# Macaron block on one Trainium2 core: a prologue put in another order, with two width tests

## The reference

```python
x = x + 0.5 * ffn(layernorm(x), ...)
x = x + mixer(layernorm(x), ...)
x = x + 0.5 * ffn(layernorm(x), ...)      # the same weights

def ffn(x):
    h = (x - mean(x)) * rsqrt(var(x) + 1e-5) * gamma + beta
    y = silu(h @ w1 + b1)                  # 256 -> 1024
    return x + 0.5 * (y @ w2 + b2)         # 1024 -> 256
# w1 and w2: (q - 128) * scales, q int32, one scale per 128 rows and column

def mixer(x):
    a = sigmoid(x @ Wa + ba); b = x @ Wb + bb; c = tanh(x @ Wc + bc)
    s[t] = a[t] * s[t-1] + (1 - a[t]) * b[t]
    return (c * s) @ Wy + by + (x @ Wd + bd)
```

## Time and profile before

| what | value |
|---|---|
| median of 3 runs | 690.57 us (689.08 to 690.64) |
| profiled execution, its own time | 690.4 us |
| its span in the profile | 687.6 us |
| granted TensorE clock over the span | 0.999 |
| TensorE, ScalarE, VectorE, GpSimd busy | 97%, 95%, 92%, 88% of the span |
| first product of fc1 on TensorE | 16.94 us |
| first scaling on ScalarE | 18.74 us |
| first product of fc2 | 25.78 us |

### The profile page before, as it was taken

The page is one execution under the profiler, slowest core; times in us unless marked ns, Lnnn a source line. Parts: engine busy times, 40 slices in busy tenths (PEclk is TensorE's granted clock), DMA queues, the critical chain, the costliest instruction groups (busy, mean ns, idle before and its releaser), DMA issues.

```text
span 687.6 us, 13669 instructions
## 1 busy us (share of the span) xinstructions
PE 668.0 (97%) x3224; PEld 539.2 (78%) x3224; DVE 634.8 (92%) x1329; ACT 653.4 (95%) x1095; POOL 604.8 (88%) x673
## 2 busy tenths in 40 slices
PE   3999999999999999999999999999999999999997
PEld 3678888888888878778877887788888888888885
DVE  5789999999999999889999998899999999999987
ACT  4899999999999999889999999999999999999994
POOL 4899999999999999857766789999999999999973
PEclk9999999999999999999999999999999999999999
DMA  8670000000000000000000000000000000000001
GB/s 254 172 236 4 1 0 0 0 0 0 0 0 0 1 0 2 1 1 1 0 0 0 0 1 1 30 33 32 31 31 31 31 31 31 31 31 32 32 32 63
DMA packets 19962, 20.22 MB, mean 29 GB/s; under 512 B 1564, under 2 KB 19666, under 8 KB 19922
## 3 DMA queue, kind: packets, MB, share of 16 engines
q1 hardware_dynamic: 19824, 19.74, 9.3%
q10 hardware_dynamic: 98, 0.02, 0.0%
HBM read 11.37 MB, written 8.39 MB: 29 GB/s over the span
## 4 chain that ended last, share of the span: by engine, by line
PE 90%; ACT 3%; DVE 3%; issue 2%; DMA 1%; ACTq 0%; POOL 0%; DVEq 0%; POOLq 0%
PE ps_z L1009 38%; PE ps_fc L1009 33%; PE ps_fc L1142 8%; PE ps_tr L1002 5%; PE ps_tr L1070 4%; PE ps_fc L1150 2%; PE ps_z L1002 1%; DMA rows<-in_L_attn_bc 1%; DVE z_acc L762 1%; ACT ps_fc L576 1%; ACT g_hi L593 1%; DVE stats L699 1%; ACT g_full L591 0%; DVE resid L887 0%; ACTq L530 0%
## 5 line engine op out<-in xcount | busy, mean ns | idle before, releaser
L410 POOL TENSOR_TENSOR g_lo<-g_full,g_hi 128x512 fp32r<-128x512 f32 x256 | 332.9, 1300 | 24.7 <-ACT g_hi L593 21.8
L762 DVE SCALAR_TENSOR_TENSOR z_acc<-ps_z,cols,z_acc 128x512 f32<-128x512 f32 (+1 forms) x449 | 322.2, 742 | 24.2 <-PE ps_z L1009 16.4
L1009 PE MATMUL ps_fc<-h_hi,q_sb 128*128 128x512 f32 x512 | 213.4, 417 | 1.4 <-ACT ps_fc L576 1.4
L1009 PE MATMUL ps_z<-g_hi,q_sb 128*128 128x512 f32 x512 | 202.4, 395 | 0.1
L1009 PE MATMUL ps_fc<-h_lo,q_sb 128*128 128x512 f32 x512 | 202.3, 395 | 0.0
L1009 PE MATMUL ps_z<-g_lo,q_sb 128*128 128x512 f32 x512 | 200.6, 392 | 0.0
L591 ACT ACTIVATE g_full<-ps_fc,safe_scale 128x512 f32<-128x512 f32 x256 | 194.8, 761 | 3.9 <-PE ps_fc L1009 2.2
L593 ACT ACTIVATE g_hi<-ps_fc,safe_scale 128x512 fp32r<-128x512 f32 x256 | 196.2, 766 | 0.0
L576 ACT ACTIVATE ps_fc<-ps_fc,bias,ratio 128x512 f32<-128x512 f32 x193 | 157.9, 819 | 1.8 <-DVE bias L873 1.8
L1009 PEld LDWEIGHTS ps_z<-g_hi,q_sb 128*128 128x128 f32 x512 | 96.1, 188 | 25.0 <-DVE z_acc L762 2.7
L1009 PEld LDWEIGHTS ps_fc<-h_hi,q_sb 128*128 128x128 f32 x512 | 97.3, 190 | 21.0 <-ACT ps_fc L576 2.1
(11 more groups left out here) (110 smaller groups left out, 820.4 us busy)
## 6 DMA issues: line engine op xcount, KB each, us to landing
resid<-in_L_attn_x SPq DMA_DIRECT2D x15, 512.0 KB, 4.6
out_x<-resid SPq DMA_DIRECT2D x15, 512.0 KB, 2.9
q_int<-in_L_ffn_fc_q SPq DMA_DIRECT2D x4, 512.0 KB, 7.3
resid<-in_L_attn_x SPq DMA_DIRECT2D x2, 256.0 KB, 3.0
out_x<-resid SPq DMA_DIRECT2D x2, 256.0 KB, 2.7
wd_sb<-in_L_attn_Wd SPq DMA_DIRECT2D x1, 256.0 KB
wy_raw<-in_L_attn_Wy SPq DMA_DIRECT2D x2, 64.0 KB
bias_rows<-in_L_attn_by SPq DMA_DIRECT2D x1, 128.0 KB
```

The lines of the kernel that those rows point to most:

```text
L410: nc.gpsimd.tensor_tensor(g_lo[:, g % 4, :], g_full[:, g % 4, :], g_hi[:, g % 4, :].bitcast(F32), ALU.subtract).then_inc(g_ready, 1)
L762: nc.vector.scalar_tensor_tensor(out=z, in0=bank_of(g, n, par)[:, tokens], scalar=col(R_S2 + KC * g + n), in1=z, op0=ALU.mult, op1=ALU.add ...
L1009: last = nc.tensor.matmul(out, w, v, start=start and i == 0, stop=stop and i == len(pairs) - 1, skip_group_check=not start)
```

## The change

The change rebuilds the prologue and the first tile's order; the other tiles, the mixer and the second feed forward keep theirs.
- The biases of the mixer leave `rows`: SP loads them straight into `mixer_cols`, in three loads ahead of `bias_rows`. `rows` isn't set to zero any more, ScalarE's queue issues six loads.
- TensorE issues matmuls on `ones` whose result nothing reads (`keep_busy`): 13 before it turns `rows`, 2 behind that, 2 before the first branch.
- The width is tested twice: over q1 alone before fc1 starts, over q1 and q2 before fc2 starts. Between them TensorE makes the first four groups of tile 0 (`opening`).
- ScalarE does its half of `xhat` before `cols`, and converts q1's second half ahead of the second `round_h`. Of q2 it converts the first half; GpSimd converts the second, behind the residual of tile 0.
- The first power (tile 0) is made in two parts, 4 columns each; the second stands behind `prepare_columns`.
- `fold_beta` uses ratios made beforehand, and sums in one reduce of five terms.
- VectorE: the reduces of q2 and the statistics and variance of tile 1 stand behind `fold_beta` and the second `lower_h`. In tile 0 all four blocks of tile 1's `xhat` are VectorE's, at f = 4 behind the scaling of group 4; statistics of tile 2 at f = 5, its variance at f = 6, statistics and variance of tile 3 at f = 7; `lower_h` at f = 6 and 7.
- GpSimd: tile 1's power stands at f = 2 of tile 0, behind `g_low` of group 1 (before: ahead of group 0); the residual at f = 5 and 6, tile 2's power at f = 6, its `xhat` at f = 7. TensorE turns tile 1 at f = 5 and 7 (before: 3 and 5).

The diff, cut to its core:

```diff
+        FIRST_TURN_AT, FIRST_LOWER_AT = (5, 7), (6, 7)
+        FIRST_RESIDUAL_AT = {5: (0, 1), 6: (2, 3)}
+        FIRST_NORMALISE_AT, FIRST_RSQRT_AT = {7: (0, 1, 2)}, 6
+
+        def first_or(ff0, before, first, usual):
+            return first if ff0 == 0 and not before else usual[before]
...
 # SP
+            for v, at, i in ((ba, 0, 0), (bb, N, 0), (bc, N, 1)):
+                sp.dma_start(mixer_cols[at:at + N, i:i + 1], v.rearrange("(n a) -> n a", a=1)).then_inc(mixer_loaded, 16)
...
 # GpSimd
-            nc.gpsimd.memset(rows[:, :], 0.0).then_inc(rows_zero, 1)
...
+            def rsqrt_first():
+                pool.wait_ge(terms_ready, 1)
+                nc.gpsimd.tensor_tensor(rstd[:, 0, :], var_terms[:, 0, 0, :], minus_half[:, 0, :],
+                                        ALU.pow).then_inc(rstd_ready, 1)
+                pool.wait_ge(rstd_ready, 1)
+                nc.gpsimd.tensor_tensor(shift[:, 0, :], rstd[:, 0, :], neg_mean[:, 0, :],
+                                        ALU.mult).then_inc(shift_ready, 1)
+
+            def rsqrt_rest():
+                nc.gpsimd.tensor_tensor(rstd[:, 1, :], var_terms[:, 0, 1, :], minus_half[:, 1, :],
+                                        ALU.pow).then_inc(rest_ready, 1)
+                pool.wait_ge(rest_ready, 1)
+                nc.gpsimd.tensor_scalar(res_scale[:, :], rstd[:, 1, :], 1.0, 1.0, ALU.mult, ALU.add)
+                nc.gpsimd.tensor_tensor(shift[:, 1, :], rstd[:, 1, :], neg_mean[:, 0, :],
+                                        ALU.mult).then_inc(rest_ready, 1)
+                pool.wait_ge(rest_ready, 2)
...
-                        elif ff0 == 0:
-                            rsqrt(ln0 + 1, 1, True)
-                        if ff0 == 0 and not before and f == 1:
-                            normalise(ln0 + 1, 1, 1, halves[0], True)
+                        if ff0 == 0 and not before and f == 2:
+                            rsqrt(ln0 + 1, 1, True, 1)
...
                 if ff0 == 0:
-                    rsqrt(ln0, 0, True)
+                    rsqrt_first()
                     normalise(ln0, 0, 0, halves[0], True)
                     prepare_columns()
+                    rsqrt_rest()
                     residual(ln0, 0, 1)
+                    pool.wait_ge(q2_loaded[1], 16)
+                    nc.gpsimd.tensor_scalar(q2_sb[:, q2_halves[1], :], q2_int[:, q2_halves[1], :], -ZERO_POINT, None,
+                                            ALU.add).then_inc(q2_ready[1], 1)
...
 # ScalarE
-            act.wait_ge(rows_zero, 1)
...
-            for v, r, at in ((ba, R_AB, 0), (bb, R_AB, N), (bc, R_C, N)):
-                act.dma_start(rows[r:r + 1, at:at + N], v.rearrange("(a n) -> a n", a=1)).then_inc(rows_loaded, 16)
...
                 if ff0 == 0:
                     normalise(ln0, 0, 0, halves[1], xhat_half_ready)
-                    convert_q1(0)
+                    act.wait_ge(rows_turned, 1)
+                    nc.scalar.activation(cols[:, :], ps_fc1[:, 3, 0:ROWS], ACT.Copy).then_inc(cols_ready, 1)
+                    act.wait_ge(cols_ready, 1)
                     for c in range(KC):
+                        convert_q1(c)
                         round_h(ln0, ff0, 0, c, bank=(ps_tr, ps_tr2)[c])
-                    convert_q1(1)
-                    for k in range(KC):
-                        act.wait_ge(q2_loaded[k], 16)
-                    nc.scalar.activation(q2_sb[:, :, :], q2_int[:, :, :], ACT.Copy,
-                                         bias=-ZERO_POINT).then_inc(q2_ready, 1)
+                    act.wait_ge(q2_loaded[0], 16)
+                    nc.scalar.activation(q2_sb[:, q2_halves[0], :], q2_int[:, q2_halves[0], :], ACT.Copy,
+                                         bias=-ZERO_POINT).then_inc(q2_ready[0], 1)
...
 # VectorE, tile 0
+                        if ff0 == 0 and not before and f == LAG:
+                            normalise(ln0 + 1, 1, 1, halves[0], xhat_ready)
+                            normalise(ln0 + 1, 1, 1, halves[1])
+                        if ff0 == 0 and not before and f == 5:
+                            dve.wait_ge(x_loaded[0], 32)
+                            dve.wait_ge(aggr_done, ln0 + 2)
+                            statistics(2)
+                        if not before and f == (3 if ff0 else 6):
                             if ff0 == 0:
-                                dve.wait_ge(x_loaded[0], 32)
-                                dve.wait_ge(aggr_done, ln0 + 2)
-                                statistics(2)
+                                dve.wait_ge(rest_ready, 2)
                             variance(ln0 + 2, 0)
-                            if ff0 == 0:
-                                normalise(ln0 + 1, 1, 1, halves[1])
-                        if not before and f == 5:
+                        if not before and f == (5 if ff0 else 7):
...
 # VectorE, prologue
-                    for k, part in enumerate(q2_halves):
-                        largest_of(KC + k, q2_int[:, part, :].rearrange("p g d -> p (g d)"), q2_loaded[k])
-                    join_largest()
-                    dve.wait_ge(scale_done, 3)
-                    nc.vector.reciprocal(inverse[:, :], safe_scale[:, :]).then_inc(ratio_ready, 1)
+                    join_largest(0, KC)
+                    prepare_ratios()
                     lower_h(ln0, ff0, 0, 0)
-                    find_width()
-                    dve.wait_ge(ratio_ready, 1)
-                    nc.vector.tensor_tensor(ratio[:, :], cols[:, R_S1:R_S1 + FC], inverse[:, :], ALU.mult)
-                    dve.wait_ge(x_loaded[1], 16)
-                    statistics(1)
-                    variance(ln0 + 1, 1)
+                    find_width(0, KC + 2)
                     dve.wait_ge(beta_done, KC)
                     fold_beta(1)
                     lower_h(ln0, ff0, 0, 1, ps_tr2)
+                    for k, part in enumerate(q2_halves):
+                        largest_of(KC + k, q2_int[:, part, :].rearrange("p g d -> p (g d)"), q2_loaded[k])
+                    join_largest(1, 2 * KC + 2)
+                    dve.wait_ge(x_loaded[1], 16)
+                    dve.wait_ge(aggr_done, 1)
+                    statistics(1, halves[0])
+                    find_width(1, 2 * KC + 4)
+                    statistics(1, halves[1])
+                    variance(ln0 + 1, 1)
                     prepare_wide()
...
 # TensorE
+            def keep_busy(count):
+                wide_ones = ones[:, :].rearrange("p (o n) -> p o n", o=1).broadcast_to([P, TILE // P, P])
+                for i in range(count):
+                    nc.tensor.matmul(ps_fc1[:, 1, :].rearrange("p (a n) -> p a n", n=P), ones[:, :], wide_ones,
+                                     start=True, stop=True)
+
+            pe.wait_ge(ones_ready, 1)
+            keep_busy(13)
             pe.wait_ge(consts_ready, 1)
-            pe.wait_ge(rows_loaded, 16 * 9)
+            pe.wait_ge(rows_loaded, 16 * 6)
...
+            def opening(narrow):
+                for f in range(LAG):
+                    half_products(0, 0, f, 0)
+                    if narrow and f == LAG - 1:
+                        turn_all_largest()
+                    if f >= 1:
+                        add_products(0, 0, f - 1, 0)
...
-            pe.wait_ge(cols_ready, 1)
+            keep_busy(2)
             for c in range(KC):
                 turn(0, 0, c, (ps_tr, ps_tr2)[c], 2, 1)
...
             beta_products(1, q1_sb).then_inc(beta_done, 1)
+            keep_busy(2)
             pe.wait_ge(flag_ready, 1)
-            wide = pe.value_load(wide_flag[0:1, 0:1], min_val=0, max_val=1)
+            q1_wide = pe.value_load(wide_flag[0:1, 0:1], min_val=0, max_val=1)
+            with pe.If(q1_wide < 1):
+                q1_parts = (q1_sb,)
+                opening(True)
...
+            pe.wait_ge(flag_ready, 2)
+            wide = pe.value_load(wide_flag[0:1, 1:2], min_val=0, max_val=1)
             with pe.If(wide < 1):
                 q1_parts, q2_parts = (q1_sb,), (q2_sb,)
                 program()
```

More of the change, by code:

```diff
@@ L104, in macaron_kernel @@
         cols = sb("cols", [P, ROWS])
+        mixer_cols = sb("mixer_cols", [P, 2])
         ident = sb("ident", [P, P])
@@ L169, in macaron_kernel @@
         q1_ready = sem("q1_ready")
-        q2_ready = sem("q2_ready")
+        q2_ready = [sem(f"q2_ready{k}") for k in range(KC)]
         beta_ready = sem("beta_ready")
@@ L632, in tile @@
                             first_sum(ff, par, 1)
-                        if (behind >= 2 or ff0 == 0) and f == 7:
+                        if ff0 == 0 and before == 1 and f == 0:
+                            normalise(ln + 1, t + 1, 1 - par, REST, xhat_half_ready)
+                        if (behind >= 2 or ff0 == 0) and (ff0 or before) and f == 7:
                             normalise(ln + 2, t + 2 if behind >= 2 else 1 - behind, par, REST, xhat_half_ready)
@@ L911, in prepare_wide, with lower_weights @@
```

(23 more changed lines are left out.)

151 lines of the change are left out of this document (85 added, 66 removed).

## The result

The changed kernel takes 697.89 us (697.21 to 699.76), the kernel before, run beside it, 690.12: ratio 1.0119, interval 1.0102 to 1.0137. The forecast was 688.0 us with a range up to 691.5; the kernel became 1.2% slower. The profiled execution has a span of 695.6 us against 687.6. In time the same two executions lie 7.0 us apart (697.42 and 690.4): the time is 1.8 us above the span here and was 2.8 above it before. With the changed prologue this excess is 1.7 to 1.9 us in every execution of every version, with the old one 2.1 to 2.8; the profile doesn't show what lies in it, and the forecast took it as constant. Three executions of the experiments, at 963, 970 and 3841 us, are slow ones and enter no ratio.

What follows compares the result with a forecast made beforehand. All engines were read as nearly full, with VectorE's stretch to tile 0's group 4 addition deciding. Of 5.35 us won at the bias 3.0 are spent and 2.35 remain: 690.4 - 2.35 = 688.05, rounded 688.0; range 686.9 to 691.5.

Steps and rivals of the forecast that it cites:

- the time of the kernel is 36.88 plus a remainder that the change leaves alone: From fc2's matmul at 36.88 us (tile 0, group 5, n = 1), TensorE runs gapless; only that start moves.
- Part 7: VectorE's stretch in tile 0, from `shift` to group 4's addition: 11.8 us, ending at 33.75 in place of 36.09.
- Parts 1 to 4: Prologue up to the first `silu`: columns at 9.1, bias at 13.3 not 18.65, silu at 15.35 not 20.87.
- rival (b): Rows land no sooner: 689.2 us; second case, landing before 7.8 wins only 0.5 more: 687.5; chance 0.08.
- Part 5: VectorE up to tile 1's variance: terms at 19.3 us; costs nothing up to 2.5 us.
- Part 6: GpSimd's added conversion of q2's half: 2.1 us, hidden up to 3.1; tile 1's `shift` at 21.9.
- Rival (a): TensorE at the lower clock through the prologue: silu of group 0 at 18.75 not 15.35, kernel 691.4 us; chance 0.20.
- (c): VectorE's stretch in tile 0 doesn't bind, so TensorE's and ScalarE's 4.8 to 5 us come through: 685.5; chance 0.05.
- (d): GpSimd's conversion is dear: delays from 3.1 us, no gain at 5.5, kernel 0.3% slower at 7.6; chance 0.03.
- (e): Second width flag reaches TensorE over 2.5 us later, delaying scaling 4: 1 us at worst, 689.0; chance 0.04.
- The step from span to time: Whole kernel: profiled execution 690.4 us, 2.8 above its span; the saving in span was taken straight off the time.
- the 2.35 us of the forecast: Net gain at tile 0's group 5 matmul: of 5.35 us won at the bias, 3.0 spent on VectorE's later work.

Runs made afterwards that it cites:

- a_layout: The changed kernel with every tensor common to both kernels at its old address, the enlarged and new ones allocated last: 693.1 us, ratio 1.0051.
- b_layout: The kernel before with every common tensor at the address the changed kernel gives it: 696.19 us, ratio 1.0098.
- a_split: a_layout_act with tile 1's `xhat` blocks 0 and 1 made by GpSimd, blocks 2 and 3 left on ScalarE: 689.57 us, ratio 1.0008.
- a_layout_act: a_layout with the four blocks of tile 1's `xhat` made by ScalarE instead of VectorE: 689.85 us, ratio 1.0007.
- a_split_late: a_split with tile 3's statistics and variance on VectorE moved from f = 7 of tile 0 into tile 1: 689.93 us, ratio 1.0001.
- a_pad32: The changed kernel with 32 bytes per partition of padding ahead of `xhat`: 696.93 us, ratio 1.0106.
- a_layout_nobusy: a_layout without the 17 filler matmuls on ones: 691.91 us, ratio 1.0031.

## Why the prediction was wrong, point by point

- **Its frame failed: "the time of the kernel is 36.88 plus a remainder that the change leaves alone".** The change moves the tensors that TensorE streams, and those around them, by 96 bytes, and 22 of the 32 tiles take 0.22 to 0.30 us more each. Between 4.8 us (a_layout) and 6.7 us (b_layout) of the 7.8 are this. The diff showed the enlarged tensors; they were given no price, and no rival had this mechanism.
- **Part 7, "Four blocks of `xhat` ... 1.35", was mis-sized: 4.21.** The row used, two blocks in 0.73, had GpSimd idle beside its first block (its `shift` ends at 20.07, its next `g_lo` starts at 22.21, when the second block already ran, and takes 1.47 us in place of 1.28); the moved blocks stand beside three `g_lo`. Taking them off VectorE went with 3.25 us less by the medians. The trace of before held a sign of it: its four-column operation on `var_terms`, line 715, takes 0.17 us at 17.56, where GpSimd is idle, and up to 0.98 in the tiles, ending with a GpSimd instruction. What GpSimd does at the new place wasn't asked. The Trainium skill, page "SBUF — State Buffer", section "Who interferes with whom", says that VectorE and GpSimd contend for one shared port pair, which is locked exclusively; the Trainium skill, page "VectorE: DVE Perf Modes", section "Mode 2×_2P — use both read ports for one tensor", names `tensor_scalar` from SBUF to SBUF as the kind that takes both ports. By that rule a block waits for GpSimd's instruction to end, and the traces agree: 1.35 us against 0.40, with each end just behind that of a `g_lo`, while additions, which have one operand in PSUM, do four in 2.71 us from 37.59 on, 0.66 apart, with GpSimd busy beside them.
- **Parts 1 to 4, the prologue: right in the main.** Columns at 8.4 (forecast 9.1; the rows landed before 7.44, when the fillers ended, which was rival (b)'s second case), bias at 12.66 (13.3), first half product 13.13. Silu of group 0 came at 16.00 (15.35), the fall of the clock in between.
- **Part 5:** statistics and variance ended at 20.6, not 19.3: the second width test held VectorE until 18.16, and `var_terms` of four columns took 0.75 us beside `g_lo`. **Part 6:** the conversion took 2.79 us (2.1), hidden as foretold. `shift` at 22.8, 0.9 late.
- **Part 7, what decides: the mechanism was right.** VectorE runs without a break to group 4's addition and TensorE waits 2.1 us for `z_acc`. In a_split, without `xhat` on VectorE and without the prologue's fall, the matmul came at 34.23 against the 34.5 that follows from the forecast; the nearness is in part luck, since VectorE there has no `xhat` to make and instead waits 0.69 and 0.56 us for others and spends 1.27 on four columns of `var_terms`. What failed there is that a wait of TensorE was priced at its length: 1.4 of the 2.65 us go to the lower clock behind it.
- **Rival (a)** was half right. The fillers raise the clock, and in this profile and those of a_layout, a_layout_act and a_split_late it falls again at 14 us for some 3 us (not in those of a_split and a_pad32). Its price, 3.4 us on the `silu` of group 0, was too high: without fillers that `silu` comes at 17.35 (a_layout_nobusy), 2.4 us behind the 14.90 and 15.02 of the two profiles that stay at the upper level. The fall behind the later waits, 27 to 31 us, it did not have. Rivals (c), (d) and (e) did not happen, and of (b) only the second case did.
- **The step from span to time**, 2.8 us taken as constant, was 1.8: 1.0 us in the change's favour, with no cause known.

Step by step on the medians: 697.89, 693.1 with the old addresses, 689.85 with `xhat` on ScalarE, within 0.3 us of the kernel before. Where the 2.35 us of the forecast went is told by two profiles. In a_split 2.65 arrive at the decisive matmul and 1.4 go to the lower clock behind the wait. In a_layout_act only 0.5 arrive, since its prologue's fall makes `silu` 1.2 us later than in a_split and `xhat` comes later still, and 1.4 go the same way. Why the prologue's fall comes in some executions and not in others was not tried.

## What to carry to other kernels

Compare the start addresses of all SBUF operands before and after an edit; if a growing tensor shifts what TensorE streams, allocate it last, or time the kernel before with an unused tensor of the same size. When an instruction that reads and writes SBUF on VectorE is moved, price it by what GpSimd runs at the new place, not by its old duration. Don't price a wait of TensorE at its length alone: six waits of 2.2 to 4.1 us in these traces were followed by a stretch at the lower level, worth 1.4 us where it can be read (a_split, a_layout_act), though one of 2.1 in a_layout_act was not; so a gain at one end that turns into such a wait is in part given back.

## What was not expected of the hardware

- Spacing of gapless 128x512 fp32r matmuls, by where `xhat`, `h`, `g` and `z_acc` together start in their partition, weights fixed at 128 mod 256: 229.0 ns at 128, 229.6 at 192, 232.8 at 160, 233.3 at 224, and at 0 mod 256 229 to 230 on the low part of each pair and 236 to 237 on the high one. With `g_full`, `g_hi`, `g_lo` and what lies behind them at 160 and `h_hi`, `h_lo` at 128, the tile was nearly as slow as with all at 160 (16.61 against 16.65), and the matmuls on the unmoved `h` slowed too. Whether the distance to the weights, to another tensor, or the address itself counts was not tried, nor which reader or writer of SBUF the matmul meets there.
- A VectorE operation of four columns took up to 1.78 us beside GpSimd's stream, 0.16 alone.
- The granted clock reads 1.00 over products that stand 0.43 us apart, where no rise had gone before (20 to 24 us in the kernel before, 14 to 17 us in a_layout_nobusy), and 0.50 over the same spacing behind a rise (14 to 17 us in the changed kernel).
- TensorE's granted clock fell in stretches full of matmuls behind a pause (27.1 to 30.7 us after, 34.6 to 37.5 in a_split, 37.7 to 40.9 in a_layout_act), 0.43 us a matmul in place of 0.23: at once in the first, 0.3 us and 1.3 us after the matmuls had begun again in the others.
